# Two mixtures and an attention in one block, the second mixture's front woven into the attention's output

## What is computed

```python
def _L0_attn_b_ref(x, wq, wk, wv, wo):
    Q, K, V = x @ wq.T, x @ wk.T, x @ wv.T
    energy = jnp.einsum('bnd,bne->bde', K, V)
    context = jnp.einsum('bnd,bde->bne', Q, energy) * sqrt(3.0 / D)
    return jnp.einsum('bnd,ed->bne', context, wo)

def _L0_ffn_ref(x, gate_w, ln_gamma, ln_beta, fc1s, b1s, fc2s, b2s):
    xf = x.reshape(-1, d)                      # 4096 x 128, 8 experts
    scores = (jnp.tanh(xf @ gate_w.T) + 1.0) * 0.5
    vals, idx = jax.lax.top_k(scores.T, k)     # k = 512 tokens of each expert
    y = _layernorm(xf[idx.T], ln_gamma, ln_beta)
    h = gelu(einsum('knd,nfd->knf', y, fc1s) + b1s)
    o = (einsum('knf,ndf->knd', h, fc2s) + b2s) * vals.T[:, :, None]
    return xf.at[idx.T].add(o)
# x = x + layer(_layernorm(x)) for mixer, ffn, attn_b, ffn
```

## Time and profile before

| | |
|---|---|
| median of 3 runs | 870.04 us (869.19 to 870.29) |
| the profiled execution | 868.72 us |
| its span | 866.4 us |
| mean granted TensorE clock | 0.853 of full speed |
| DVE / ACT / POOL busy | 585.9 / 485.7 / 568.5 us |

### The profile page before, as it was taken

One profiled execution on the slowest core, in us unless ns is written; L12 is line 12 of the kernel. 1 busy time (PEld: TensorE's weight loads), 2 busy tenths in 40 slices (PEclk: granted clock), 3 DMA queues, 4 the chain that ended last, 5 costly groups with the idle time before them and its releaser, 6 DMA issues. The chain is left out here.

```text
span 866.4 us, 11675 instructions
## 1 busy us (share of the span) xinstructions
PE 643.0 (74%) x3819; PEld 481.7 (56%) x3819; DVE 585.9 (68%) x1101; ACT 485.7 (56%) x915; POOL 568.5 (66%) x443
## 2 busy tenths in 40 slices
PE   6779997899978999788876655689443861289942
PEld 4247765786767866676665434466332740266731
DVE  6368899888999889999994778523115568843300
ACT  2279789776888768898770586223113159213211
POOL 6029899888999889999994300778860020078875
PEclk8978999899988999999899665599786975569967
DMA  5034556444444455545541704523334004323332
GB/s 148 1 118 154 172 168 173 150 158 174 152 173 146 163 168 159 168 159 184 180 166 45 219 1 103 146 42 41 39 28 107 1 1 103 98 55 42 41 40 24
DMA packets 68697, 95.59 MB, mean 110 GB/s; under 512 B 15289, under 2 KB 48866, under 8 KB 68642
## 3 DMA queue, kind: packets, MB, share of 16 engines
q1 hardware_dynamic: 56818, 85.19, 30.9%
q0 software_dynamic: 11264, 8.66, 7.6%
q10 hardware_dynamic: 560, 1.05, 0.4%
HBM read 81.73 MB, written 13.11 MB: 109 GB/s over the span
## 5 line engine op out<-in xcount | busy, mean ns | idle before, releaser
L361 POOL TENSOR_TENSOR product<-state,c_all 128x1024 f32<-128x1024 f32 x128 | 301.1, 2375 | 31.8 <-issue 14.8
L462 ACT ACTIVATE decay<-dt,decay_rate 128x1024 f32<-128x1024 f32 x128 | 143.9, 1142 | 22.0 <-DVE state L616 19.8
L880 POOL DMA_INDIRECT f_got<-f_table,f_tokens x64 | 65.3, 1021 | 134.5 <-DVE f_tokens L1301 118.3
L616 DVE TENSOR_TENSOR_SCAN state<-decay,carry,m_psum 128x1024 f32<-128x1024 f32 x64 | 147.6, 2337 | 5.7 <-ACT decay L462 1.7
L616 DVE TENSOR_TENSOR_SCAN state<-decay,m_psum 128x1024 f32<-128x1024 f32 x64 | 144.5, 2280 | 10.1 <-issue 3.4
L780 PE MATMUL m_psum<-ident,product 128*128 128x128 f32 x1024 | 141.4, 285 | 4.3 <-POOL product L361 4.3
L780 PEld LDWEIGHTS m_psum<-ident,product 128*128 128x128 f32 x1024 | 121.0, 147 | 18.9 <-issue 10.6
L1149 ACT ACTIVATE f_f_T<-f_psum,shared_b_T 128x512 f32<-128x512 f32 x64 | 44.0, 687 | 152.8 <-PE f_psum L1465 152.8
L440 ACT ACTIVATE drive_T<-dtu_T,b_T 128x128 f32<-128x128 f32 x352 | 111.0, 392 | 10.1 <-PE m_psum L804 9.5
L804 PE MATMUL m_psum<-ident,drive_T 128*128 128x128 f32 x608 | 88.6, 293 | 22.2 <-DVE state L616 22.2
L804 PEld LDWEIGHTS m_psum<-ident,drive_T 128*128 128x128 f32 x608 | 75.6, 152 | 42.6 <-DVE state L616 30.5
(11 more groups left out here) (202 smaller groups left out, 964.3 us busy)
## 6 DMA issues: line engine op xcount, KB each, us to landing
c_all<-c_dram SPq DMA_DIRECT2D x128, 512.0 KB, 4.0
f_table<-f_rows SPq DMA_DIRECT2D x2, 2176.0 KB, 9.4
X<-in_L_attn_a_x SPq DMA_DIRECT2D x4, 512.0 KB, 7.6
f_w_raw<-in_L_ffn_fc2s SPq DMA_DIRECT2D x1, 2048.0 KB, 16.5
between<-f_f SPq DMA_DIRECT2D x1, 2048.0 KB, 10.0
X<-between SPq DMA_DIRECT2D x4, 512.0 KB, 6.0
out<-f_f SPq DMA_DIRECT2D x1, 2048.0 KB, 8.9
carry<-state SPq DMA_DIRECT2D x64, 0.5 KB, 2.2
```

What stands on the lines that cost most here:

```text
L361: pool.tensor_tensor(product[:, n % RING, :], state[:, n % RING, :], c_all[:, n % RING, :], ALU.mult).then_inc(product_ready, 1)
L462: act.activation(decay[:, n % RING, :], dt[:, k, :], ACT.Exp, scale=decay_rate[:, k, s:s + 1]).then_inc(decay_ready, 1)
L616: dve.tensor_tensor_scan(state[:, n % RING, :], decay[:, n % RING, :], pair(n).rearrange("p a t -> p (a t)"), 0.0 if starts_batch(g) else ...
L880: pool.indirect_dma_start(got[:, e, t, :], None, table, bass.IndirectOffsetOnAxis(ap=tokens[:, e, t:t + 1], axis=0)).then_inc(gathered[e], 16)
```

## The change

One block holds f1, the attention and f2. Each of the three functions now returns one function per engine, and `build` calls them one behind the other on each engine. `room_of` makes one set of buffers for both mixtures and the attention (`f`, `f_T` and PSUM are shared; the raw first-layer weights lie in `got`, so POOL waits for `w_taken` before the gathers). The constants are made once. The front is cut out as `front_of`, works in quarters of 8 tiles, and takes two strings: `makers` names the engine that normalises each tile (a ACT, d DVE, p POOL), `takers` the one that copies each turned group. The front of f2 is called from the attention's lists. The attention's outputs use three PSUM banks where they used four. The base's store waits for expert 0's gathers. The attention's weights are loaded with the mixture's.

```diff
+def front_of(nc, ctx, name, X, f, f_T, psum, banks, scores, gate_pad, makers, takers):
+    QT = TILES // 4
...
+    def scale(dve, q):
+        dve.wait_ge(std_done, q + 1)
+        dve.reciprocal(rstd[:, tiles], rstd[:, tiles]).then_inc(inverse, 1)
...
+    def normalise(engine, by, q):
+        engine.wait_ge(scaled, q + 1)
+        for i in range(QT * q, QT * (q + 1)):
+            if makers[i] != by:
+                continue
...
+    def gate(pe, g):
+        pe.wait_ge(taken[takers[g]], takes(g))
...
             sp.wait_ge(base_ready, TILES)
+        sp.wait_ge(gathered[0], 16 * KT)
         sp.dma_start(dst.rearrange("(i p) d -> p i d", p=P), f[:]).then_inc(base_stored, 16)
...
+    def gpsimd(pool):                      # attention
+        for q in range(4):
+            front["normalise"](pool, "p", q)
...
-            for n in range(4):
-                link_copy(1, n)
-                add(n)
-            for g in range(4, NB):
-                add(g)
+        for n in range(4):
+            link_copy(1, n)
+            if n < 3:
+                add(n)
+        dve.wait_ge(added, 2)
+        front["measure"](dve, 0)
+        add(3)
+        front["scale"](dve, 0)
+        add(4)
+        dve.wait_ge(added, 4)
+        front["measure"](dve, 1)
+        add(5)
+        front["scale"](dve, 1)
...
+        add(7)
+        dve.wait_ge(added, 8)
+        front["measure"](dve, 3)
+        front["scale"](dve, 3)
+        front["normalise"](dve, "d", 3)
+        front["variance_again"](dve)
+        for g in (6, 7):
+            front["take"](dve, "d", g)
+        front["scale_again"](dve)
...
+        for q in range(3):
+            front["root"](act, q)
+            front["normalise"](act, "a", q)
+            if q:
+                front["take"](act, "a", 2 * q - 2)
+                front["take"](act, "a", 2 * q - 1)
+        front["root"](act, 3)
+        front["normalise"](act, "a", 3)
+        front["take"](act, "a", 4)
+        front["take"](act, "a", 5)
+        front["root_again"](act)
+        act.preload_act_table(ACT.Tanh)
+        front["tanh"](act)
...
+        output(5)
+        front["turn"](pe, 1, ident)
+        output(6)
+        front["gate"](pe, 0)
+        output(7)
+        for g in range(2, NB + 1):
+            if g < NB:
+                front["turn"](pe, g, ident)
+            front["gate"](pe, g - 1)
...
+            front_1 = front_of(nc, rest, "f1", X, room["f"], room["f_T"], room["psum"], (0, 1, 2, 3, 0, 1, 2, 3), 4,
+                            room["gate_pad"], "a" * 8 + "aaaaaaaa" + "aaaaapap" + "aapdapda", "aaaaaadd")
+            front_2 = front_of(nc, rest, "f2", X, room["f"], room["f_T"], room["psum"], (4, 5, 7, 6, 4, 5, 7, 6), 3,
+                            room["gate_pad"], "apaapaap" * 3 + "apdapdad", "aaaaaadd")
```

More of the change, by code:

```diff
@@ L844, in moe, with mixture @@
+def mixture(nc, X, ident, room, front, name, dst, first_use, reloaded, gate_w, ln_gamma, ln_beta, fc1s, b1s,
+            fc2s, b2s):
     E, FF, DM = fc1s.shape
@@ L1477, in attention @@
-def attention(nc, X, ident, x_loaded, wq, wk, wv, wo):
+    SHARE = (20, 3, 3, 2, 2, 2, 0, 0)
+    assert MIDDLE <= 2048 and HALVES == 2 and sum(SHARE) == E * KT
+    COUNTS, PLACES, LISTS, W_TURN, SMALL = 0, 1, (2, 3, 2, 7), 5, 7
+    YT, HID, OUT = 0, 2, 6
+    table = nc.dram_tensor(f"{name}_table", [T, ROW], F32, kind="Internal").ap()
+    psum, search = room["psum"], front["search"]
+    gamma, b1_T, b2_all, gate_pad, w1_T, w2_T = (
+        room["gamma"], room["b1_T"], room["b2_all"], room["gate_pad"], room["w1_T"], room["w2_T"])
@@ L1483, in attention @@
+    return sync, gpsimd, scalar, vector, tensor, load
+def attention(nc, ctx, X, ident, room, front, x_loaded, wq, wk, wv, wo):
     HD, DM = wq.shape
@@ new lines, in attention, with sync, gpsimd @@
+    fT_ready = sem("fT_ready")
+    small_turned = sem("small_turned")
+    small_ready = sem("small_ready")
+    gram_summed = sem("gram_summed")
+    link = sem("link")
+    linked = sem("linked")
+    out_ready = sem("out_ready")
+    added = sem("added")
+    QT = TILES // 4
+    def sync(sp):
+        for out, what in ((q_w[:], wq), (kv_w[:, 0, :], wk), (kv_w[:, 1, :], wv), (o_w[:], wo)):
+            sp.dma_start(out, what).then_inc(loaded, 16)
+    def gpsimd(pool):
+        for q in range(4):
+            front["normalise"](pool, "p", q)
@@ new lines, in scalar, with root, normalise, take_turned @@
+    def scalar(act):
+        def root(h):
+            part = slice(h * TB, (h + 1) * TB)
+            act.wait_ge(variance, h + 1)
+            act.activation(rstd[:, part], rstd[:, part], ACT.Sqrt).then_inc(std_done, 1)
+        def normalise(first, end):
+            for i in range(first, end):
+                act.activation(f[:, i, :], X[:, i, :], ACT.Identity, bias=shift[:, i:i + 1],
+                               scale=rstd[:, i:i + 1]).then_inc(f_first, 1)
+        def take_turned(g):
+            act.wait_ge(turned, g + 1)
+            act.copy(f_T[:, g * BANK:(g + 1) * BANK], psum[:, g % 4, :]).then_inc(fT_ready, 1)
+        act.preload_act_table(ACT.Sqrt)
+        root(0)
+        act.wait_ge(ln_ready, 2)
+        normalise(0, TB // 2)
+        root(1)
+        take_turned(0)
+        normalise(TB // 2, 3 * TB // 4)
+        take_turned(1)
+        normalise(3 * TB // 4, TB)
+        for g in range(2, NB):
+            take_turned(g)
+        for q in range(3):
[4 more added lines that the diff above has]
+                front["take"](act, "a", 2 * q - 1)
+        front["root"](act, 3)
+        front["normalise"](act, "a", 3)
+        front["take"](act, "a", 4)
+        front["take"](act, "a", 5)
+        front["root_again"](act)
+        act.preload_act_table(ACT.Tanh)
+        front["tanh"](act)
@@ L1688, in build @@
+    return sync, gpsimd, scalar, vector, tensor
 def build(nc, inputs, out):
```

1521 lines of the change are left out of this document (778 added, 743 removed).

## The result

| | before | changed |
|---|---|---|
| median of 4 runs | 869.96 us (869.19 to 870.29) | 859.94 us (855.18 to 863.88) |
| the profiled execution, its span | 868.72 us, 866.4 us | 862.87 us, 861.1 us |
| ratio, with its 95% interval | | 0.9874 (0.9833 to 0.9914) |

A forecast was written before the change was run, and what follows sets the result against it. Behind the mixer it saw a row of stages, each with its own limit: POOL's list in the expert stages, no engine above 70% in the fronts. -2.6 -1.35 -0.5 -6.0 = -10.4 us gave 859.6 us; eight in ten 856.0 to 865.0.

The forecast's parts named there:

- base's store behind gathers, f1: f1's expert stage: first four gathers undisturbed, POOL's 2.78 us wait for DVE before its first scatter goes; -2.6 us.
- one block, X's reload: Attention's start: without the boundary DVE starts on eight tiles, then is limited by X's second quarter; -1.35 us.
- f1's front in quarters: f1's front: same work in another order, first normed tiles 2.4 us sooner; -0.5 us, between -1.5 and +1.
- f2's front in the output: f2's front woven under the attention's output, mix's copy to score rounding; -6.0 us, bounds 1.0 and 7.9 us of gain.
- f2's stage: f2's expert stage: the store moves from a free place but has about 5 us of cover; no gain or loss.
- The walk: f2's front stepped through four engine lists from the second mix's copy: rounding at 708.5 or 710.2, before 715.6.
- The first: Rival: PE at half clock or queue order leaves f2's front 1 to 4 us; some 863 us in all; 22%.
- The second: Rival: boundaries and waits cost more than rows name; f2's front gives 8, f1's front 1.5; 856.5 us; 18%.
- The fourth, a late store: Rival: POOL's first scatter and DVE's first bias wait for the base's store in both mixtures; 874 us at 22; 4%.
- The third: Rival: the weave does nothing or is given back to a wait elsewhere in the attention; -4, 866 us; 6%.
- GpSimd in DVE's way: f2's front: DVE's scale, three tiles and second variance may each wait for a 0.6 us POOL operation; 0 to 1.5 us.
- hardly any other wait: Both expert stages before: POOL's operations each have 0.3 us of issue and little other waiting; its list sets the cost.

The follow-up runs named there:

- f1_halves: The changed kernel with f1's front in the old order (16 statistics ahead of each scale, makers by halves): ratio to before 0.9854, f1's front 23.67 us.
- same: The changed kernel run once more, unaltered: ratio to before 0.9893, median 860.74 us, 378.5 us behind the mixer.
- store_later: The changed kernel with the base's store waiting for expert 1's gathers too: ratio to before 0.9890, f1's stage 105.9 us.
- no_pool: The changed kernel with GpSimd's tiles in f2's front normalised by ACT: ratio to before 0.9953, mix's copy to rounding 27.96 us.
- warm: The changed kernel with extra PE products whose results nobody reads: ratio to before 0.9839, median 855.84 us, mix's copy to rounding 22.91 us.
- gate_late: The changed kernel with PE doing output 7 ahead of gate 0: ratio to before 0.9842, median 856.07 us, mix's copy to rounding 21.75 us.
- before_again: The kernel before run once more, unaltered, for its trace: 389.1 us behind the mixer, f1's stage 107.5 us.
- store_free: The changed kernel with the base's store no longer waiting for expert 0's gathers: ratio to before 0.9894, median 860.29 us, f1's stage 107.1 us.

## Why the prediction was right

By its own steps, in microseconds:

| term | forecast | measured |
|---|---|---|
| base's store behind gathers, f1 | -2.6 | -2.5 in the profile; 2.5 to 3.0 put into before, 1.7 to 1.9 taken out; 2.0 to 2.5 by the place of the first scatter |
| one block, X's reload | -1.35 | -1.3 |
| f1's front in quarters | -0.5 (-1.5 to +1) | -1.6, and -2.8 to -1.5 over all executions with quarters |
| f2's front in the output | -6.0 (-1.0 to -7.9) | -6.8 behind the mix's copy in the profile; -5.0 there from the first statistic on, -5.1 on the mean of five executions |
| f2's stage | 0 | +0.4 in the profile (855.75 less 750.02, against 105.36); 105.0 to 105.7 over all executions of changed kernels |
| sum | -10.4 | -10.4 in the profile, -10.5 on the means of two executions each |

The profiled pair adds up by stages: f1's front -1.6, f1's stage -2.5, from its last scatter to the attention's first statistic -1.7 (7.37 for 9.04), from there to f2's rounding -5.0, f2's stage +0.4, together -10.4; f2's search (-0.3) and what lies behind the last scatter (+0.3) cancel.

**The store** was right in size and in mechanism, and both ways round. It ended the wait that it was said to end, at the place that was named.

**The reload** came out by 0.03 us: DVE starts on eight tiles and then hangs on the second quarter of X.

**f1's front** is the term that was mis-sized. I walked it with "both ways together ... leave a small gain", from durations at the clock of before. What I left out is PE's clock in this front. The order in quarters gives PE its tiles sooner, and in all ten executions with it the clock rose 3 to 7 us sooner than in before. The length of the front goes with that moment; that the earlier rise is what shortens it is read from the rows, since no run raised the clock alone, and one and the same list saw it rise at 9.6 us in six executions and at 12.6 in three. f1_halves puts the quarters at 0.8 to 2.1 us; 0.7 us remain even in halves (24.36 less 23.67), which I did not take apart.

**f2's front.** The walk holds step by step in the changed kernel. Counted from the end of the mix's copy: copy of group 0 done at 10.0 (walked 10.35), output 7 at 12.0 (12.15 with PE fast), the copy of group 4 at 17.8 (17.85), rounding at 23.05 (22.75). The other four executions with this order gave 24.10 to 24.91; the walk had 24.45 with PE slow at output 7, and the rows of `same` show it there at half clock, 1.92 us for an output that takes 1.05. In the changed kernel's profile the slow clock fell elsewhere: into the attention ahead of the copy, and under outputs 5 and 6, for which nobody waited. Hence -6.8 in one column and only -5.0 when counted from the first statistic. Over the five executions stat to round is 52.0 to 52.8 us, 52.4 on the mean, against 57.5. From the first statistic to the mix's copy it is now 27.6 where it was 27.34 (with the clock up), because the statistics wait for the second quarter; that 0.3 belongs to the reload. So the weave, the quarters and the missing boundary are worth 5.4 us, where I put 6.0. The -6.0 gave 0.6 less than forecast and the -0.5 gave 1.1 more; that the sum came to -10.4 is luck in that part, since the -1.6 lies outside the range that I gave f1's front (-1.5 to +1).

**The rivals.** The first (queue order eats the gain) was a true mechanism at a small price: gate 0 ahead of output 7 cost 1.2 to 1.3 us at full clock, more with PE at half, and the walk had it in. The second (more than walked) was right about f1's front (-1.6 for its -1.5) and wrong about the larger term (8 for 5.4). The fourth, a late store, falls: store_later moved its issue by 5.9 us more and nothing waited. It also took for granted that all four gathers under the old store were slowed by more than twice; they landed in 3.2, 4.5, 6.6 and 6.1 us. The third falls by the rows. GpSimd in DVE's way, which I bounded by 0 to 1.5 us, cost about 0.1: the second variance (L900) took 0.27 us beside GpSimd's last tiles, and 0.19 in no_pool, where GpSimd does nothing. It ended at 704.02, and GpSimd's tiles (from 702.98 on, 1.01 us) at 703.99. The same meeting stands in all nine executions with GpSimd's tiles in f2's front, 0.27 us each and ending 0.03 to 0.04 us behind GpSimd. The Trainium skill, "SBUF — State Buffer", section "Who interferes with whom", has an operation with two SBUF inputs contend with one of GpSimd's that reads SBUF; whichever issues first holds the shared ports, and the other waits until it is over. These meetings agree with it, though they met only the end of GpSimd's work. In f1's front another doesn't: there L900 starts within 0.01 us of a GpSimd tile, and takes 0.20 us while that tile runs on for its usual 0.45. What GpSimd brought was much more: without its tiles mix to round is 3 to 5 us longer in PE's order of the change, and up to 3.4 in the other (25.16 less 21.75, part of it the clock).

Two readings of before were slightly off, and nothing rests on them. DVE was busy for 17.43 of the 24.80 us of f1's front, 70.3% and not at most 70%. And POOL's list in the expert stages has "hardly any other wait" only up to its last fifth, where two waits of some 2.5 us stand in both mixtures.

What stays open: why the mixer's end scatters by 8 us, why PE's clock fell inside the attention in two of eleven executions and not in the others, and what the reload in one block and the boundary that is gone give by themselves; both are read from rows, and no run takes out one alone.

## What to carry to other kernels

When two stages are woven, look on each queue for the item that waits longest, and see whether something that another engine needs stands behind it; moving one output ahead of one gate gave 1.2 to 1.3 us, where the whole weave gave some 4. A large store that lies among small gathers delays the first of them; let it wait until the consumers of these have started, and measure the cover that it has. Before two spans are compared, find the moment at which the changed code begins in each: here 5.1 us of scatter in code that nobody had touched hid half of a gain of 10.4.

## What the runs showed of the hardware

- The same list of instructions found PE at another clock level in different executions. Between 682 and 686 us the changed kernel's PE was at 0.50 to 0.66 (1.2 GHz and its way back to 2.4), and eight products of an output took 1.98 us; in `same`, with the same list of instructions, they took 1.11.
- PE idle for 2.6 us ahead of gate 0 was followed by half clock in `same` (0.79, then 0.50) and by full clock in warm, where three products of 256 columns had filled an earlier gap. In gate_late, without such products, 1.7 us of idle time ahead of gate 0 were followed by full clock as well.
- Of f1's first four gathers in before, the one issued 2.8 us ahead of the 2 MB store landed in 3.2 us and the other three in 4.5 to 6.6; with no store beside them f2's took 2.5 to 3.2. The store itself took 8.7 to 8.9 us with no gathers beside it (f2 in before, before_again and store_free) and 9.1 to 10.5 everywhere else.
- In f1's front, PE came to full clock some 9.6, 12.6 to 13.1, or 16 to 16.5 us behind the start, and the front took 21.5 to 22.3, 22.8 to 22.9, and 23.7 to 24.4 us.
- A DVE operation on 32 columns with two SBUF inputs took 0.27 us beside the end of a GpSimd tile, in nine executions, and 0.18 to 0.19 where GpSimd was idle; begun together with a tile, in f1's front, it took 0.20.
